# Cross attention of a six-stage decoder on one core: the turned scores made by a second product instead of transposes

## What is computed

```python
def _L1_xattn_ref(query, key_value, Wq, bq, Wk, bk, Wv, bv, Wo, bo):
    ...
    scale = D ** (-0.5)
    q = (query @ Wq + bq).reshape(B, Nq, H, D).transpose(0, 2, 1, 3)
    k = (key_value @ Wk + bk).reshape(B, Nkv, H, D).transpose(0, 2, 1, 3)
    v = (key_value @ Wv + bv).reshape(B, Nkv, H, D).transpose(0, 2, 1, 3)
    attn = jnp.einsum('bhqd,bhkd->bhqk', q, k) * scale
    attn = jnp.clip(attn, -CLAMP, CLAMP)
    attn = jax.nn.softmax(attn, axis=-1)
    ...
    x = jnp.einsum('bhqk,bhkd->bqhd', attn, v).reshape(B, Nq, Cq)
    return x @ Wo + bo
```

## Time and profile before

| | us |
|---|---|
| median of 3 runs | 1396.94 |
| lowest and highest | 1391.53, 1397.68 |
| the profiled execution, its time | 1399.06 |
| the profiled execution, its span | 1397.2 |
| TensorE busy (matmuls) | 1284.8 |
| VectorE busy | 910.7 |
| ScalarE busy | 594.0 |
| GpSimd busy | 750.8 |

### The profile page before, as it was taken

How to read it: one execution, slowest core, us unless ns; L and a number is a source line. 1 busy time by engine, 2 the same in 40 slices (tenths; PEclk the granted TensorE clock), 3 DMA queues, 4 the chain that set the end, 5 groups by cost and what they waited for, 6 DMA issues and landing times.

```text
span 1397.2 us, 23666 instructions
## 1 busy us (share of the span) xinstructions
PE 1284.8 (92%) x9077; PEld 1091.0 (78%) x9077; DVE 910.7 (65%) x2279; ACT 594.0 (43%) x1218; POOL 750.8 (54%) x697
## 2 busy tenths in 40 slices
PE   6997899999999999999999999999883999999991
PEld 6996688888888888887777777777663899999991
DVE  4666622552262244223578888989985979999993
ACT  3567411121121112113454555555442767777763
POOL 3543556576666657653221224433445448888883
PEclk9999999999999999999999999999995999999996
DMA  6101233333343324321343343345543757677755
GB/s 193 37 24 35 61 97 99 99 109 103 113 131 103 91 76 119 93 82 28 104 130 94 86 140 103 100 127 150 145 174 108 249 155 224 178 235 234 225 119 139
DMA packets 67664, 171.51 MB, mean 123 GB/s; under 512 B 10601, under 2 KB 36297, under 8 KB 59616
## 3 DMA queue, kind: packets, MB, share of 16 engines
q1 hardware_dynamic: 52576, 122.29, 29.0%
q0 software_dynamic: 14976, 47.72, 12.2%
HBM read 136.51 MB, written 35.56 MB: 123 GB/s over the span
## 4 chain that ended last, share of the span: by engine, by line
PE 58%; DVE 25%; issue 5%; POOL 4%; DMA 4%; ACT 3%; SPq 1%; ACTq 0%; POOLq 0%; DVEq 0%
PE bank L463 13%; PE bank L465 13%; PE bank L464 13%; PE bank L471 5%; DVE w_lo L1958 4%; PE bank L1203 3%; DVE gh_hi L2042 3%; PE bank L1122 3%; DVE w_lo L1960 3%; DVE shiftE L1896 2%; PE bank L1190 2%; DVE shiftE L1890 2%; DMA sum_rows<-yblock,row_out 2%; PE bank L1216 2%; PE bank L1281 1%
## 5 line engine op out<-in xcount | busy, mean ns | idle before, releaser
L1756 DVE CAST hid_hi<-bank 128x512 fp32r<-128x512 f32 x96 | 66.4, 691 | 256.5 <-ACT bank L1481 255.4
L609 POOL TENSOR_TENSOR wpiece_lo<-wraw,wpiece_hi 128x1024 fp32r<-128x1024 f32 x88 | 212.3, 2412 | 7.3
L463 PE MATMUL bank<-hid_hi,wpiece_lo 128*128 128x512 f32 x512 | 201.4, 393 | 0.0
L465 PE MATMUL bank<-hid_hi,wpiece_hi 128*128 128x512 f32 x512 | 201.1, 393 | 0.0
L464 PE MATMUL bank<-hid_lo,wpiece_hi 128*128 128x512 f32 x512 | 201.1, 393 | 0.0
L607 POOL TENSOR_SCALAR wpiece_hi<-wraw 128x1024 fp32r<-128x1024 f32 x88 | 94.1, 1070 | 156.2 <-PE bank L465 129.8
L1481 ACT ACTIVATE bank<-bank,ffn_scales 128x512 f32<-128x512 f32 x64 | 42.4, 662 | 306.0 <-PE bank L465 306.0
L463 PE MATMUL bank<-xgT_hi,w_lo 128*128 128x256 f32 x368 | 108.4, 295 | 8.8 <-DVE xgT_lo L1966 8.3
L463 PEld LDWEIGHTS bank<-hid_hi,wpiece_lo 128*128 128x128 f32 x512 | 96.3, 188 | 22.0 <-DVE hid_lo L1758 0.8
L465 PEld LDWEIGHTS bank<-hid_hi,wpiece_hi 128*128 128x128 f32 x512 | 96.3, 188 | 21.5
L464 PEld LDWEIGHTS bank<-hid_lo,wpiece_hi 128*128 128x128 f32 x512 | 96.3, 188 | 21.3
(11 more groups left out here) (348 smaller groups left out, 3603.4 us busy)
## 6 DMA issues: line engine op xcount, KB each, us to landing
wraw<-in_C_w SPq DMA_DIRECT2D x88, 512.0 KB, 3.6
w2raw<-in_F_w SPq DMA_DIRECT2D x8, 1152.0 KB, 8.0
w1raw<-in_F_w SPq DMA_DIRECT2D x8, 1028.0 KB, 7.6
split_qk<-qk_hi SPq DMA_DIRECT2D x64, 128.0 KB, 2.4
xt_lo<-split_qk SPq DMA_DIRECT2D x8, 1024.0 KB, 4.9
xt_hi<-split_qk SPq DMA_DIRECT2D x8, 1024.0 KB, 5.4
split_qk<-qk_lo SPq DMA_DIRECT2D x32, 128.0 KB
split_qk<-ctx_raw SPq DMA_DIRECT2D x32, 128.0 KB, 2.4
```

The costliest lines, as they stand in the source:

```text
L463: pe.e.matmul(o, sl, mh, start=start and i == 0, stop=False)
L465: made = pe.e.matmul(o, sh, mh, start=False, stop=stop and i == n - 1)
L609: pool.e.tensor_tensor(pair[1], raw, f(pair[0]), ALU.subtract).then_inc(done, 1)
```

## The change

A pair now goes as follows. TensorE makes the scores as before. VectorE takes one negated maximum over each of the four rows of 256 columns, straight from the double bank, and bounds the four maxima (`topE`); the scores themselves are not written to SBUF. A round later ScalarE makes four tiles `diagE` of 128x128 from the identity, each with the maxima of 128 queries on its diagonal. TensorE multiplies the scores a second time with the operands exchanged, so that keys are on partitions, into two single banks, and leaves the sums open. VectorE bounds these in place, one instruction a bank. TensorE then adds to each bank the product of a 128x128 tile of ones with the diagonals, twice a bank, each diagonal read two times by a zero step; that takes every query's maximum off its column. ScalarE's exponential follows. No transpose of scores is left. The steps get the rounds 0, 2, 2, 4 in place of 0, 2, 4; the diagonals, the turned products and the bounds in place are step 1, ones with diagonals and the exponential step 2, with priority `SHIFT_AT`, products with values step 3.

```diff
--- before.py
+++ after.py
@@ -109,9 +109,10 @@
     return in_rounds(items)
 
 
+SHIFT_AT = 3.5
 PLACE = {
     "all": {("DPRE", 1): 0.5, ("EDR", 0, 0): 1.5, ("EFIN", 3): -1, ("EFIN", 5): 2.5, ("EPRE", 2): 1.5, ("EPRE", 3):
-            3.5, ("PAIR", 1): 0.5, ("PAIR", 2): -0.5, ("QUAD", 0): 4.5, ("QUAD", 2): -2, ("SLOTS", 0): -1, ("XT", 0):
+            3.5, ("PAIR", 1): 0.5, ("PAIR", 3): -0.5, ("QUAD", 0): 4.5, ("QUAD", 2): -2, ("SLOTS", 0): -1, ("XT", 0):
             0.5},
     "dve": {("EFIN", 2): 3.5, ("EFIN", 6): 0.5, ("PAIR", 0): 0.5},
     "pool": {("EFIN", 1): -0.5, ("EFIN", 6): -2},
@@ -134,7 +135,7 @@
         items += [(d + 7 + 4 * c, (5, -1)[c], "DDR", (b, c), 1) for c in range(KC)]
         items.append((d + 11, (5, 4.5, 2.5, 5), "DFIN", (b,), 4))
         items.append((d + 12, 5, "EPRE", (b,), (0, 1, 3, e + 1 - d - 12)))
-        items += [(e + p, (0, 1, 2), "PAIR", (b, p), (0, 2, 4)) for p in range(PAIRS)]
+        items += [(e + p, (0, 1, SHIFT_AT, 2), "PAIR", (b, p), (0, 2, 2, 4)) for p in range(PAIRS)]
         items += [(e + 8 + 4 * c, 5, "EDR", (b, c), 1) for c in range(KC)]
         items.append((e + 13, 5, "EFIN", (b,), (0, 1, 2, 4, 4, 5, 7, 8 if b == B - 1 else 9)))
         items.append((e + (21 if b == B - 1 else 23), 6, "SLOTS", (b,), 2 * TT))
@@ -212,7 +213,7 @@
             out.append((("E", "s", *args), wide_e))
         elif name == "PAIR" and step == 1:
             out += [(("E", "p", *args, i), upper) for i in range(2)]
-        elif name == "PAIR" and args[1] % 2:
+        elif name == "PAIR" and step == 3 and args[1] % 2:
             out.append((("E", "a", args[0], args[1] // 2), upper))
         elif name in ("DFIN", "EFIN"):
             key = {0: "c", 1: "o", 3: "x", 5: "l", 7: "r"}.get(step)
@@ -394,7 +395,7 @@
         qk_lo = [sbp("qk_lo0", [P, KC, S], F32R), ctx_room[1].bitcast(F32R)]
         q_e, k_e = ([x[:, i, :].rearrange("p (j s) -> p j s", j=PAIRS) for i in range(2)] for x in (xt_hi, xt_lo))
         top_e = ring(3, lambda i: sbp(f"topE{i}", [P, 2 * TT]))
-        shift_e = ring(3, lambda i: sbp(f"shiftE{i}", [P, 2 * TT, S]))
+        diag_e = ring(3, lambda i: sbp(f"diagE{i}", [P, 2 * TT, P], F32R))
         prob_e = [stage_room[:, i * 4 * S:(i + 1) * 4 * S].rearrange("p (i k s) -> p i k s", i=2, k=TT) for i in range(3)]
         xtf = sbp("xtf", [P, KC, S])
         rt = ring(2, lambda i: sbp(f"route{i}", [P, TT, 13, NE]))
@@ -409,6 +410,7 @@
         s_dwo, s_ew = sem("dwo"), sem("ew")
         s_xb, s_cthi = {k: sem(f"xb_{k}") for k in "DE"}, {k: sem(f"ct_hi_{k}") for k in "DE"}
         s_shift, s_shared = sem("e_shift"), sem("f_shared")
+        s_turned, s_diag = s_nm, s_phi
         s_qkhi, s_qklo, w_qk, l_qk = sem("e_qkhi"), sem("e_qklo"), ring(2, lambda i: sem(f"w_qk{i}")), ring(2, lambda i: sem(f"l_qk{i}"))
         s_rm, s_re, s_rf, s_rb, s_rs, s_sh = (sem(f"r_{n}") for n in ("m", "e", "f", "b", "s", "sh"))
         s_seen, s_slot = sem("r_seen"), sem("r_slot")
@@ -919,7 +921,7 @@
                                 load(held[i, r], f(src[i * 4 * DH:(i + 1) * 4 * DH, :, :]).rearrange("p c s -> p (c s)"), w_qk[which])
                 sp.wait_ge(w_qk[which], 16 * 8 * (b + 1))
                 if b >= 2:
-                    old = use["E", "s", b - 2, PAIRS - 1]
+                    old = use["E", "p", b - 2, PAIRS - 1, 1]
                     sp.wait_ge(old.filled, old.full)
                 load(f((q_e if which else k_e)[b % 2]).rearrange("p j s -> p (j s)"),
                      held.rearrange("i r (d j) s -> (i r d) (j s)", j=4), l_qk[b % 2])
@@ -1260,15 +1262,30 @@
                     made.then_inc(u.filled, 1)
                 elif name == "PAIR" and step == 1:
                     b, p = args
+                    pair = [use["E", "p", b, p, i] for i in range(2)]
+                    for u in pair:
+                        pe.wait_ge(u.drained, u.turn)
+                    for kt in range(TT):
+                        for i, u in enumerate(pair):
+                            rows = slice(i * 4 * DH, (i + 1) * 4 * DH)
+                            pe.e.matmul(u.ap[:, kt * S:(kt + 1) * S], k_e[b % 2][rows, p, kt * P:(kt + 1) * P],
+                                        q_e[b % 2][rows, p, :], start=kt == 0, stop=False,
+                                        skip_group_check=True).then_inc(s_turned, 1)
+                elif name == "PAIR" and step == 2:
+                    b, p = args
                     n = b * PAIRS + p
-                    pe.wait_ge(s_shift, n + 1)
+                    pe.wait_ge(s_rtmem, 2)
+                    pe.wait_ge(s_diag, B + n + 1)
                     for i in range(2):
                         u = use["E", "p", b, p, i]
-                        pe.wait_ge(u.drained, u.turn)
-                        transposes(pe, [(u.ap[:, kt * S + t * P:kt * S + (t + 1) * P],
-                                         shift_e[n % 3][:, i * TT + t, kt * P:(kt + 1) * P])
-                                        for kt in range(TT) for t in range(TT)]).then_inc(u.filled, 1)
-                elif name == "PAIR" and args[1] % 2:
+                        pe.wait_ge(s_shift, 2 * n + i + 1)
+                        o = u.ap[:, :].rearrange("p (k s) -> p k s", k=TT)
+                        for t in range(TT):
+                            made = pe.e.matmul(o[:, :, t * P:(t + 1) * P], ones_r[:, :],
+                                               diag_e[n % 3][:, i * TT + t, None, :].to_broadcast([P, TT, P]),
+                                               start=False, stop=t == TT - 1, skip_group_check=True)
+                        made.then_inc(u.filled, 1)
+                elif name == "PAIR" and step == 3 and args[1] % 2:
                     b, p = args
                     n, u = b * PAIRS + p, use["E", "a", b, p // 2]
                     pe.wait_ge(use["E", "v", b].drained, use["E", "v", b].done)
@@ -1556,6 +1573,16 @@
                     made.then_inc(u.drained, 1)
                 elif name == "PAIR" and step == 1:
                     b, p = args
+                    n, u = b * PAIRS + p, use["E", "s", b, p]
+                    act.wait_ge(u.drained, u.done)
+                    if n >= 3:
+                        old = use["E", "p", *divmod(n - 3, PAIRS), 1]
+                        act.wait_ge(old.filled, old.full)
+                    for m in range(2 * TT):
+                        made = act.e.activation(diag_e[n % 3][:, m, :], ident[:, :], ACT.Identity, scale=top_e[n % 3][:, m:m + 1])
+                    made.then_inc(s_diag, 1)
+                elif name == "PAIR" and step == 2:
+                    b, p = args
                     n = b * PAIRS + p
                     act.wait_ge(s_ew, 4)
                     if n >= 3:
@@ -1566,7 +1593,7 @@
                         act.wait_ge(u.filled, u.full)
                         act.e.activation(prob_e[n % 3][:, i, :, :], u.ap[:, :].rearrange("p (k s) -> p k s", k=TT), ACT.Exp,
                                          scale=scale_e).then_inc(u.drained, 1)
-                elif name == "PAIR" and step == 2 and args[1] % 2:
+                elif name == "PAIR" and step == 3 and args[1] % 2:
                     b, p = args
                     keep_sums("E", b, p // 2)
                 elif name == "EFIN":
@@ -1884,17 +1911,17 @@
                     scores = u.ap[:, :].rearrange("p (m s) -> p m s", s=S)
                     dve.wait_ge(u.filled, u.full)
                     if n >= 3:
-                        old = use["E", "p", *divmod(n - 3, PAIRS), 1]
-                        dve.wait_ge(old.filled, old.full)
-                    for m in range(2 * TT):
-                        made = dve.e.tensor_scalar(shift_e[n % 3][:, m, :], scores[:, m, :], lim, -lim, ALU.min, ALU.max,
-                                                   accum_out=top[:, m:m + 1])
-                    made.then_inc(u.drained, 1)
-                    dve.wait_ge(u.drained, u.done)
-                    for m in range(2 * TT):
-                        sh = shift_e[n % 3][:, m, :]
-                        made = dve.e.tensor_scalar(sh, sh, -lim, top[:, m:m + 1], ALU.max, ALU.subtract)
-                    made.then_inc(s_shift, 1)
+                        dve.wait_ge(s_diag, B + n - 2)
+                    dve.mark(dve.e.tensor_reduce(top[:, :], scores, AX.X, ALU.max, negate=True))
+                    dve.wait_own()
+                    dve.e.tensor_scalar(top[:, :], top[:, :], lim, -lim, ALU.min, ALU.max).then_inc(u.drained, 1)
+                elif name == "PAIR" and step == 1:
+                    b, p = args
+                    n = b * PAIRS + p
+                    for i in range(2):
+                        u = use["E", "p", b, p, i]
+                        dve.wait_ge(s_turned, B + 4 * n + 3 + i)
+                        dve.e.tensor_scalar(u.ap[:, :], u.ap[:, :], lim, -lim, ALU.min, ALU.max).then_inc(s_shift, 1)
                 elif name == "EFIN":
                     b, = args
```

## The result

The changed kernel takes 1461.99 us (median of 4 runs, 1457.31 to 1468.52), the kernel before 1397.31 us beside it (4 runs, 1391.53 to 1398.83): 1.0471 times, 95% interval 1.044 to 1.0501. The forecast was 1410 us with a range up to 1431. The direction held, the size didn't.

What follows compares the result with a forecast made beforehand. TensorE was taken to bound from 741 to 934 us, VectorE from 984 to 1045 us. Terms 0 + 0 + 10 + 1 + 2 = +13 us on 1396.94 gave about 1410 us, range 1380 to 1431 us.

Steps and rivals of the forecast that it cites:

- five bare rounds: Rounds with no products between turned product and ones product: TensorE goes on 2.0 us later in each, +10 us.
- covered: Six of eight kinds of round have 1.4 to 3.1 us of products hiding the 1.3 us clipping: no loss.
- x_tok adds: Rounds like 836.60 us, beside GpSimd's adds: 1.0 us later, but a 1.07 us wait goes; four 0, fifth +1 us.
- second regime: Stretch from 984 to 1045 us, VectorE bounds: sixteen pairs lose 0.35 us each, less 3.4 us, +2 to +3 us.
- TensorE work: Per pair, eight transposes go (0.92 us) and eight products come (0.92 us): nothing gained or lost.
- VectorE work: Per pair 2.55 us before; one wide maximum, a small bound and two wide bounds after, 2.55 us: nothing.
- slow subtractions: VectorE's subtractions slowed while GpSimd adds on x_tok; should go as new wide lines use banks only: 11 us of VectorE's time.
- ScalarE, 83 us that do "not bound": Four new diagonals a pair, 1.3 us, 83 us in all; ScalarE busy 142 of 193 us, so not the bound.
- first rival: Faster across the pairs: VectorE loses 11 us of stalls, perhaps 10 us more; 1386 or 1376 us; chance 0.28.
- third rival: Slower by more: late exponentials hold banks, last 24 pairs lose 1 us each, or half-rate operand; 1425 to 1440 us; chance 0.20.
- first regime: Stretch from 741 to 934 us, TensorE busy 188.35 of 193 us and bounding; five bare rounds there +10 us.
- no VectorE operation of the pairs at three times its median: Sign that the forecast is right: in the pairs, no VectorE operation takes three times its median.

Runs made afterwards that it cites:

- e3: Changed kernel without the bound of the turned scores and with diagonals made for the first three pairs only: 1387.29 us, ratio 0.9924.
- e1: Changed kernel with the bound of the turned scores left out: 1414.7 us, ratio 1.014.
- e12: Changed kernel with linear attention's feature products ahead of the ones products, and exponentials ahead of casts that wait for VectorE: 1437.59 us, ratio 1.0299.
- e2: Changed kernel with the diagonals made for the first three pairs only, bounds kept: 1451.89 us, ratio 1.0385.
- e4: Kernel before, with TensorE waiting once per sequence, ahead of pair 4's transposes, for VectorE's bounding of the next pair's scores: 1428.9 us, ratio 1.023.
- e9: Kernel before with one added TensorE wait per sequence, ahead of pair 4's transposes, and twenty unused products in front of it: 1416.74 us, ratio 1.0153.
- e5: Changed kernel with the linear attention's feature products ahead of the ones products and exponentials, every second round: 1454.99 us, ratio 1.0396.

## Why the prediction was wrong

The loss can be set against the sum round by round (a round runs from one pair's first score product to the next one's; the first 39 rounds, up to pair 40, then the last 24):

| part | forecast, us | measured, us |
|---|---|---|
| five bare rounds | +10 | +14.9 |
| ten rounds behind the scores of a sequence's second and third pair | 0 (covered) | +16.9 |
| the other 24 rounds up to pair 40, with those of the x_tok adds | 0 | +0.3 |
| the 24 rounds from pair 40 on | +3 | +24.8 |
| ahead of the first pair, and behind the last | 0 | -1.7, +4.9 |

So three steps failed, each below in its place: later exponentials were put at nothing in rounds that were called covered, the second regime was far too cheap, and no term stood for the lower clock.

*TensorE work, 0: right.* Ones products over a zero-step operand start 0.12 us apart at full clock, at 282 ns each, and e3, which runs all of them, is busy 184.5 us from pair 8 to 40 where the kernel before is 188.65.

*VectorE work, 0: right.* Forecast 1.25, 0.15 and twice 0.69 us; measured 1.21, 0.17 and twice 0.69. The 512 instructions fewer saved little: VectorE's busy time fell by 4.5 us over the whole program (910.7 to 906.2), less than the 11 us that the prediction counted for the slow subtractions alone.

*The slow subtractions, 11 us: half right.* They are gone, but the bound on the four maxima, priced at 0.15 us, reads and writes SBUF like the subtraction did, and is slow beside GpSimd in its turn (timeline of GpSimd and VectorE in the changed kernel):

```profile
748.12 1.26 POOL L611 TENSOR_TENSOR ctx_lo<-ctx_raw,ctx_hi 96x512 fp32r<-96x512 f32 x1
748.24 1.17 DVE L1917 TENSOR_SCALAR topE<-topE 128x4 f32<-128x4 f32 x1
```

Four elements per row take 1.17 us and end as GpSimd's operation does, 0.03 us after it. The mean of line 1917 is 257 ns against 170 in the undisturbed case, so 64 of them cost 5.6 us more than they would undisturbed. Size does not decide: the bound of 512 columns in a bank, the same operation, never took over 700 ns and the wide maximum never over 1220; the one at 747.00 us took 1.21 us although GpSimd was at work from 747.42 us on. That lines which work on banks alone are spared, the prediction assumed without a row; these times bear it out. Why, no run shows.

*ScalarE, 83 us that do "not bound": right in size (81.4), wrong in the conclusion.* The step that failed reads "Cover: it needs only the maxima, which are made a round earlier", and with it the next one, that exponentials and copies come "each 1.3 us later where ScalarE has no slack", which got a term in the bare rounds alone. The prediction looked at the share of busy time, 142 of 193 us. The engine is in the loop, so what counts is when its diagonals and exponentials come and not how busy it is. The ten rounds that cost 16.9 us hold four waits of 1.5 to 2.5 us for exponentials, three by the products with v and one, at 714.30 us, by the turned products for their banks. Some 7 us of the 16.9 stay even in e1 and e3, so not all of it comes from the bounds and diagonals. Behind pair 40 TensorE waits 14.2 us for diagonals, and e12 shows 12 to 14 us in the order of ScalarE's list alone. The diagonals are a part of it and not the whole: without them e2 gains 10 us.

*The bare round, +2.0 us: the wait was right, the term was not.* TensorE goes on 1.66 us later in the round shown, forecast 2.0. The sum had no term for what follows a wait, 2.94 us at the lower clock in this round. The working read durations at full clock in every row; the earlier trace rows show 0.92 in the last 61 us, where TensorE waited, and the text passed over it. That round costs 4.6 us (9.96 against 5.36), all five 14.9 instead of 10. e4 and e9 show that what comes on top of the waits is the clock.

*The rounds of the x_tok adds, 0 and +1: too low.* TensorE waits 0.74 us before the ones there, four times, forecast 1.0. Each of these rounds takes 1.1 us more, and the next one only 0.3 less (8.44 to 8.15 us, behind the round of 836.60 us), though the 1.07 us wait for `xd_lo` is gone from it as forecast: four times 0.8 us instead of 0. The fifth, at pair 40, takes 3.2 us more (4.54 to 7.70), with a wait of 1.33 us and the lower clock behind it. The prediction also took the earlier trace rows for idle time of TensorE's products; its 5.6 us count the weight loads with them, and the products alone waited 0.8 us for the subtraction there. So the first rival had less to win than it says.

*The second regime, +0.35 us a pair: wrong by a factor of three.* It is (127.8 - 103.0) / 24 = 1.03 us a pair, and it begins at pair 40, not at 48. The third rival had this price, 1 us for each of the last 24 pairs, and the coupling through three engines. Its way was another: banks held by a late exponential. Behind pair 40 the turned products waited for one only once, 0.7 us (and once long before, 2.5 us at 714.30 us); the ones products waited, for diagonals and bounds. It came to 1425 to 1440 us because it, too, added nothing for the clock and left the first regime at +11; the first 39 rounds lost 32 us.

Of the marks named, those of the mechanism came: the diagonals and bounds at their forecast durations, idle time before the ones released by the bounds (1.1 us in the first bare round, 1.5 in the others). One didn't, "no VectorE operation of the pairs at three times its median": line 1917 is at seven times.

## What to carry to other kernels

When a step that ran a round ahead becomes a step inside the round (TensorE to another engine and back), list every round with what stands between the two ends, and price an uncovered wait at the wait plus work behind it at the lower clock: here 6.1 us of waiting in four rounds cost 13.6 us, from nothing on top of the wait to 3.1 us. An engine at 60% busy can still be waited for if the loop passes through it (ScalarE, 138.04 of 219.90 us from pair 8 to 40: TensorE's products with v waited 4.6 us there for its exponentials), so cost its new work by its place in the list; and when one link is covered, look for the next link that comes late (e5, then e12). Before doubting the new instructions, take away the step that is waited for: e3 showed that the rest of the new arithmetic was a gain of 10 us, under a loss of 75.

## What the runs showed of the hardware

TensorE's granted clock fell to its lower level behind single waits of 1.5 and 2.6 us amid otherwise dense work, and in the rounds shown it stayed there for 3.4 us (e4, 0.50 from 836.80 to 840.20 us) and 6.8 us (changed kernel, 0.50 from 893.50 to 900.30 us), with 256-column products 0.21 us apart instead of 0.12. It did not do so each time: of seven waits of 1.5 us between pair 8 and 40 two, at 784.64 and 815.45 us, were followed by none of it. Products whose result nobody needs, put ahead of the wait, kept it up (1.00 against 0.72 behind the wait) and made the kernel 12 us faster (e9 against e4, 1416.74 and 1428.9 us), though TensorE did more. A moving operand that repeats by a zero step ran at the rate of a plain one, a median of 282 ns for 256 columns, where line 465 took 281 on average before the change (741 to 934 us). And an operation on 128x4 elements in SBUF took 1.17 us instead of 0.17 and ended as GpSimd's did, while the wide maximum and the bounds, which work on banks, took at most 1.22 and 0.70 us each.
